# Start-up fill issued by two engines, maxima by pairs in the lone batches, and feed-forward chunks two places later, in an attention plus feed-forward kernel

## What is computed

```python
Q, K, V = (proj(W) for W in (Wq, Wk, Wv))      # 16 heads of 16, T = 512
att = einsum('bhqd,bhkd->bhqk', Q, K) * 0.25 + b
att = softmax(att * m + (1 - m) * -1e30)
y = einsum('bhqk,bhkd->bhqd', att, V)          # back to [8, 256, 512]
gate, up = y @ Wg.T, y @ Wu.T                  # Wg, Wu [4096, 512], Wd [512, 4096]
out = x + (gelu_tanh(gate) * up) @ Wd.T        # packed 4-bit codes times block scales
```

## Time and profile before

| what | us |
|---|---|
| median of 3 runs (1523.91 to 1530.12) | 1525.85 |
| the profiled execution | 1526.61 |
| its span, first to last instruction | 1524.8 |
| first scores of batch 0 | 62.3 |
| first gate matmul of chunk 0 | 221.8 |
| PE busy over the span | 1421.5 (93%) |
| mean granted TensorE clock, share of full | 0.966 |

### The profile page before, as it was taken

How to read it: one execution, slowest core, us unless ns; L and a number is a source line. 1 busy time by engine, 2 the same in 40 slices (tenths; PEclk the granted TensorE clock), 3 DMA queues, 4 the chain that set the end, 5 groups by cost and what they waited for, 6 DMA issues and landing times.

```text
span 1524.8 us, 18901 instructions
## 1 busy us (share of the span) xinstructions
PE 1421.5 (93%) x7376; PEld 555.1 (36%) x7376; DVE 698.3 (46%) x934; ACT 752.1 (49%) x855; POOL 309.6 (20%) x242
## 2 busy tenths in 40 slices
PE   3688779999999998999999998999999999999998
PEld 1122223333333333333433333333333334444443
DVE  5667668777778753433344333433343111111111
ACT  2255558666667663555665554556655631111110
POOL 3002024433444421111211111111111111111110
PEclk7589989999999999999999999999999999999999
DMA  5130324443354332432243320432222223233220
GB/s 182 51 87 15 101 78 163 154 131 122 108 183 157 133 125 65 143 99 84 84 128 106 101 84 20 155 119 83 84 84 83 84 83 138 83 126 123 83 84 28
DMA packets 51129, 157.91 MB, mean 104 GB/s; under 512 B 7632, under 2 KB 21072, under 8 KB 50912
## 3 DMA queue, kind: packets, MB, share of 16 engines
q1 hardware_dynamic: 48192, 153.80, 29.5%
q10 hardware_dynamic: 2848, 2.90, 0.6%
HBM read 118.64 MB, written 37.77 MB: 103 GB/s over the span
## 4 chain that ended last, share of the span: by engine, by line
PE 81%; DMA 4%; DVE 3%; ACT 3%; issue 3%; POOL 2%; SPq 2%; ACTq 1%; POOLq 0%; DVEq 0%
PE psum L896 14%; PE psum L897 13%; PE psum L898 13%; PE psum L944 8%; PE psum L945 7%; PE psum L946 7%; PE psum L866 7%; PE psum L852 4%; PE psum L836 4%; PE psum L812 2%; DMA wide<-seed_rows 2%; POOL dq_w L400 1%; DVE w_ring L414 1%; PE psum L822 1%; ACTq L393 1%
## 5 line engine op out<-in xcount | busy, mean ns | idle before, releaser
L633 ACT ACTIVATE big<-psum 128x1024 f32<-128x1024 f32 x256 | 260.1, 1024 | 328.4 <-PE psum L852 321.4
L896 PE MATMUL psum<-y_hi,w_ring 128*128 128x512 f16 x1024 | 390.5, 381 | 16.5 <-POOL y_lo L515 15.8
L898 PE MATMUL psum<-y_hi,w_ring 128*128 128x512 f16 x1024 | 389.6, 380 | 0.0
L897 PE MATMUL psum<-y_lo,w_ring 128*128 128x512 f16 x1024 | 389.4, 380 | 0.0
L700 DVE TENSOR_REDUCE maxima<-psum 128x2 f32<-128x1024 f32 x179 | 219.2, 1225 | 253.6 <-PE psum L836 253.3
L527 POOL TENSOR_TENSOR in_lo<-inter,in_hi 128x512 f16<-128x512 f32 x128 | 150.4, 1175 | 811.1 <-ACT in_hi L615 810.5
L748 DVE SCALAR_TENSOR_TENSOR inter<-psum,gelu 128x512 f32<-128x512 f32 x128 | 88.2, 689 | 315.4 <-PE psum L898 301.4
L944 PE MATMUL psum<-w_ring,in_hi 128*128 128x512 f16 x512 | 195.5, 382 | 7.7 <-ACT gelu L608 4.3
L945 PE MATMUL psum<-w_ring,in_hi 128*128 128x512 f16 x512 | 194.8, 380 | 0.0
L946 PE MATMUL psum<-w_ring,in_lo 128*128 128x512 f16 x512 | 194.6, 380 | 0.0
L896 PEld LDWEIGHTS psum<-y_hi,w_ring 128*128 128x128 f16 x1024 | 100.1, 98 | 202.6 <-issue 82.7
(11 more groups left out here) (69 smaller groups left out, 987.3 us busy)
## 6 DMA issues: line engine op xcount, KB each, us to landing
w_ring<-w_parts SPq DMA_DIRECT2D x96, 768.0 KB, 7.2
w_parts<-w_ring SPq DMA_DIRECT2D x32, 768.0 KB, 3.3
dq_scales<-scales SPq DMA_DIRECT2D x32, 384.0 KB
wide<-qk_parts SPq DMA_DIRECT2D x64, 128.0 KB
qk_parts<-wide SPq DMA_DIRECT2D x60, 128.0 KB
dq_packed<-packed SPq DMA_DIRECT2D x32, 192.0 KB
small<-x SPq DMA_DIRECT2D x8, 512.0 KB, 6.6
wide<-qk_parts SPq DMA_DIRECT2D x64, 64.0 KB
```

The lines of the kernel that those rows point to most:

```text
L633: nc.scalar.activation(p_exp[:, k, :, i], p_score[:, bank:bank + 2, :], ACT.Exp, scale=SCORE_SCALE).then_inc(exp_done, 1)
L896: nc.tensor.matmul(dst, w[:, 0, k % 2, cols], hi, start=(k == 0), stop=False)
L897: nc.tensor.matmul(dst, w[:, 0, k % 2, cols], lo, start=False, stop=False)
L898: return nc.tensor.matmul(dst, w[:, 1, k % 2, cols], hi, start=False, stop=(k == TT - 1))
```

## The change

1. **Start.** The loads of feed-forward units 0 and 1 go behind the first `move_max`; the 1792 KB mask load and its reduction go, in their place 8 values (`any_b`) go to DRAM and back to all partitions. ACT makes one tiny copy early. K's store of unit 0 goes to ACT; the first fill no longer waits for V and `x_lo`, and its ten DMAs are issued half by SP and half by ACT, after ACT's three weight splits. Fill of unit 1 comes right behind, once the first has landed (before: step `F1`). `weight_f`, `weight_hi`, `weight_lo` and `decode` of unit 0 leave the start and go into batch 0.
2. **Lone batches.** `PLAN` gets the order of `SHARED_PLAN` without places; maxima by pairs in the same two banks (4 and 5), scores stay in four. `F0` goes from the third quad to the second, `G1` from the fourth to the third. Batch 1 now decodes units 1 and 2, batch 0 unit 0.
3. **Chunks.** Each chunk starts behind the second `|` after that `YN`; two places are added at the end.
4. **End.** The last group's down products run unit by unit (i outside, r inside), and down waits for each unit's `in_lo` by itself.

```diff
         PLAN = (
-            "F1 A2 m A3 m AO m S00 S01 V1a m m S10 V1b V1h m S11 m Y S20 MT MH XH YN m m ML S21 MV A0 m m A1 m "
-            "S30 m S31 m Q0a m Q0b m Q0h Q0l",
...
-            "S00 m S01 d2 m A2 m m V0b S10 V0h m m A3 m AO S11 m MT m S20 m Y YN MH m ML U G1 S21 MV m S30 A0 m S31 m "
-            "A1 m wh m wl",
+            "S00 m m A2 V1a S01 m m A3 V1b V1h AO S10 m m XH S11 m m d10 MT Y MH ML YN d11 S20 m m A0 Q0a MV d12 S21 m m "
+            "Q0b Q0h h1 S30 m m A1 Q0l K0a S31 m m K0b K0h K0l l1",
+            "X F0 S00 m m A2 Q1a S01 m m A3 Q1b Q1h AO S10 m m Q1l S11 m m MT Y MH ML YN S20 m m A0 MV K1a S21 m m "
+            "K1b K1h S30 m m A1 K1l S31 m m",
+            "G1 S00 m m A2 d00 d20 S01 m m A3 AO S10 m m d01 d21 S11 m m MT Y MH ML YN d02 d22 S20 m m A0 MV L2 S21 m m V0a "
+            "S30 m m h0 h2 A1 V0b V0h S31 m m l0 l2",
+            "S00 m m A2 S01 m m A3 AO S10 m m S11 m m MT Y MH ML YN S20 m m A0 MV L3 S21 m m S30 m m A1 S31 m m",
         )
...
-            for step in "| A2 | A3 | AO | | Y | YN".split():
+            for step in "| A2 | A3 | AO | | Y | YN | |".split():
...
-                for r in range(4):
-                    for i in range(GROUP):
+                for i in range(GROUP):
+                    for r in range(4):
                         yield STEPS, "D", (STEPS // GROUP - 1, r, i)
...
-            ready = [n + 1 for n, (b, g, step, _) in enumerate(steps) if step == "YN" and g == 0 and b >= 2 and b % 2 == 0]
+            ready = []
+            for n, (b, g, step, _) in enumerate(steps):
+                if step == "YN" and g == 0 and b >= SOLO and b % 2 == 0:
+                    places = [m for m in range(n, len(steps)) if steps[m][2] == "|"]
+                    ready.append(places[1] + 1)
...
-            load_unit(sp, 0)
-            load_unit(sp, 1)
+            sp.wait_ge(dve_own, 2)
+            sp.dma_start(any_dram, any_b).then_inc(any_out, 16)
             sp.wait_ge(setup, 4)
             sp.wait_ge(fixed, 2)
             sp.dma_start(seed_dram, seed).then_inc(seed_out, 16)
             store_qk(sp, 0, 0, 0)
-            store_qk(sp, 0, 0, 1)
+            sp.wait_ge(seed_out, 16)
+            sp.wait_ge(qk_out[0], 64)
+            fill_half(sp, 0, 0, 0, 0)
+            store_qk(sp, 0, 1, 0)
+            store_qk(sp, 0, 1, 1)
+            sp.wait_ge(stack_in[0], 16 * STACK_DMAS)
+            fill_stack(sp, 0, 0, 1, False)
             sp.wait_ge(x_lo_s, 1)
             sp.wait_ge(v_proj, 1)
             load_x(sp, 1)
-            sp.wait_ge(seed_out, 16)
-            fill_stack(sp, 0, 0, 0, False)
+            sp.wait_ge(any_out, 16)
+            sp.dma_start(any_key[:, :], any_dram.rearrange("b o -> (b o)").partition_broadcast(P)).then_inc(any_in, 16)
             move_max(sp, 0, 0, 0)
+            load_unit(sp, 0)
+            load_unit(sp, 1)
...
             act.wait_ge(any_set, 1)
-            for u in range(2):
-                for side in range(2):
-                    qk_part(0, side, u, True, psum[:, 2 * u + side, :])
+            for side in range(2):
+                qk_part(0, side, 0, True, psum[:, side, :])
+            store_qk(act, 0, 0, 1)
+            for side in range(2):
+                qk_part(0, side, 1, True, psum[:, 2 + side, :])
+            for i in range(3):
+                act.wait_ge(proj_in[i], 16)
+                nc.scalar.activation(w_parts[i][0], w_proj[i], ACT.Copy, scale=W_SCALE).then_inc(wp_hi_s, 1)
+            act.wait_ge(seed_out, 16)
+            act.wait_ge(qk_out[0], 64)
+            fill_half(act, 0, 0, 0, 1)
...
             def down(j, r, i):
                 u = GROUP * j + i
+                if r == 0:
+                    pe.wait_ge(in_lo_s, u + 1)
                 if i == 0:
-                    if r == 0:
-                        pe.wait_ge(in_lo_s, GROUP * j + GROUP)
```

More of the change, by code:

```diff
@@ L133, in up_bank, with score_bank @@
             return psum[:, 1 if u > LAST_CHUNK and u % 2 else 3, :]
+        def score_bank(b, i):
+            return 2 * i if b < SOLO else 0
         def out_bank(j, r):
@@ L147, in build @@
         dve_own = sem("dve_own")
+        act_own = sem("act_own")
+        warm_in = sem("warm_in")
         any_set = sem("any_set")
@@ L240, in plan @@
                     continue
-                if step == "F1" and not first:
+                if step[0] in "dhl" and (step[1] == "0") != first:
+                    continue
+                if step == "L2" and not first or step == "L3" and first:
                     continue
@@ L540, in _ @@
                     x_low(b + 1)
-                elif step == "d2" and b < SOLO:
-                    weight_f(pool, b + 1)
+                elif step in ("d02", "d12", "d22") and b < SOLO:
+                    weight_f(pool, int(step[1]))
         @block.scalar
@@ L591, in _ @@
             x_high(0)
-            for i in range(3):
-                act.wait_ge(proj_in[i], 16)
-                nc.scalar.activation(w_parts[i][0], w_proj[i], ACT.Copy, scale=W_SCALE).then_inc(wp_hi_s, 1)
-            store_qk(act, 0, 1, 0)
-            store_qk(act, 0, 1, 1)
-            weight_hi(act, 0)
             max_part(0, 0, True)
@@ L621, in _ @@
                         inter_high(u - 1)
-                    elif step == "G1" and SOLO < u + AHEAD_UNITS - 1 < UNITS:
+                    elif step == "G1" and AHEAD_UNITS <= u + AHEAD_UNITS - 1 < UNITS:
                         weight_hi(act, u + AHEAD_UNITS - 1)
@@ L649, in _ @@
                     x_high(b + 1)
-                elif step == "wh" and b < SOLO:
-                    weight_hi(act, b + 1)
+                elif step in ("h0", "h1", "h2") and b < SOLO:
+                    weight_hi(act, int(step[1]))
         @block.vector
         def _(dve):
+            nc.vector.memset(act_warm[:, :], 0.0).then_inc(warm_in, 1)
             for e in range(2):
@@ L765, in _ @@
                         decode(dve, n, int(step[1]))
-                    elif step == "G3" and SOLO < n - 1 < UNITS:
+                    elif step == "G3" and AHEAD_UNITS <= n - 1 < UNITS:
                         weight_lo(dve, n - 1)
@@ L786, in _ @@
                 elif step[0] == "d" and b < SOLO:
-                    decode(dve, b + 1, int(step[1]))
-                elif step == "wl" and b < SOLO:
-                    weight_lo(dve, b + 1)
+                    decode(dve, int(step[1]), int(step[2]))
+                elif step in ("l0", "l1", "l2") and b < SOLO:
+                    weight_lo(dve, int(step[1]))
         @block.tensor
@@ L847, in scores @@
                     pe.wait_ge(max_in, 16 * MAX_DMAS * (4 * b + g) + 16 * MAX_DMAS)
+                if (b, g, k, i) == (0, 0, 0, 1):
+                    pe.wait_ge(qk_lo, 4)
                 wait_from(pe, exp_done, n - 1 if b < SOLO else n)
-                bank = 2 * i if b < SOLO else 0
                 for e in range(2):
                     rows, s = slice(HALF * e, HALF * e + STACK_ROWS), 2 * g + i
-                    last = nc.tensor.matmul(p_score[:, bank + e, :], k_stack[rows, side, s, k * P:(k + 1) * P],
+                    last = nc.tensor.matmul(psum[:, score_bank(b, i) + e, :], k_stack[rows, side, s, k * P:(k + 1) * P],
                                             q_stack[rows, side, s, :], start=True, stop=True)
```

102 lines of the change are left out of this document (43 added, 59 removed), and 4 rows, old and new, of the table PLAN.

## The result

The changed kernel takes 1530.86 us (median, 1528.01 to 1535.98) where the kernel before, run beside it, takes 1526.22: ratio 1.0032, 95% interval 1.0021 to 1.0042. The forecast was 1496. It is slightly slower, not 2% faster. Its profiled execution has a span of 1530.9 us, the one of before 1524.8, so 6.1 us have to be found.

What follows compares the result with a forecast made beforehand. PE was taken as the bound from 221.8 us, with only its waits to save. Gains of 7.2 + 3.1 - 0.6 + 14.4 + 1.7 + 4.3 = 30.1 gave 1496 us against the median, range 1489 to 1504.

Steps and rivals of the forecast that it cites:

- The step that failed: Shared stretch from 221.8 us: PE is the bound and only its waits can be saved; inside chunk 0 no loss was forecast.
- Lone batches: Batches 0 and 1 were to take 69.5 and 71.5 us against 72.55 and 70.94: gain 3.1 and -0.6.
- Rival A: Lone batches: the pair's round trip leaves PE waiting in every step and brings half clock, slower; chance 0.03 in full.
- Rival B: Lone batches: clock swings in a third of the stage or DVE's extras cost double, batches of 77, 1510 us; chance 0.16.
- Rival C: First fill limited by the issuer, so 2.4 us sooner, and lone batches of 66.5: 1486 us; chance 0.13.
- rival D: Chunk starts don't fill and the `y_lo` wait only moves, so 12 us come back: 1508 us; chance 0.05.
- First gate: Start of chunk 0: a score step, one pair and A0 go into the 4.75 us wait, gain 1.7.
- Start: Up to the second transpose of maxima: earlier first fill, then costlier pairs, second transpose at 65.6 not 72.80, gain 7.2.
- the second issuer: First fill issued by two engines: saves at most 2.4 us of issue time, and nothing was taken for it.
- Chunk starts: Chunks 1 to 3: the wait for `y_lo` is filled by feed-forward steps of the chunk before, gain 14.4.
- End: Last group's down products: PE no longer waits 2.72 us for `in_lo` nor restarts at half clock, gain 4.3.
- PE's waits in the shared stretch: Sign of a wrong prediction: these waits growing beyond the 4 us in 320 of before.

Runs made afterwards that it cites:

- e1: Changed kernel with part 3 undone, every chunk starting right behind YN again: 1520.03 us, ratio 0.9961 to the kernel before.
- e3: Kernel before with part 3 alone, chunks starting two places later: 1536.53 us, ratio 1.0068 to the kernel before.
- e5: Changed kernel with chunk 0 starting right behind YN and keeping its old step counts, chunks 1 to 3 still later: 1509.24 us, ratio 0.9896.
- e12: Changed kernel with lone pairs in four banks, chunks three places later, unit 1 decoded in batch 0's last quad: 1484.22 us, ratio 0.9722.
- e7: Changed kernel with maxima one tile at a time in the start and lone batches: 1516.23 us, ratio 0.9928 to the kernel before.
- e9: Changed kernel with lone maxima by pairs in turn in four banks, scores in two: 1513.53 us, ratio 0.9923 to the kernel before.
- e8: Changed kernel with both halves of the first fill issued by SP alone: 1532.44 us (one run).
- e4: Changed kernel with POOL splitting y at step S21, not YN, in quads from batch 2 on that start no chunk: 1524.95 us, ratio 0.9995.

## Why the prediction was wrong, step by step

In the spans the forecast was 30.1 us less and the measurement is 6.1 more, 36.2 apart: 21.7 and 1.7 in and ahead of chunk 0, 8.7 in the lone batches, 3.1 inside chunks 1 and 2, 2.0 at the chunk starts, less the start, better by 0.9, and the end, by 0.1.

1. **The step that failed.** It is the sentence "Nothing in the change removes a feed-forward matmul, so there only its waits can be saved". It says what can be gained and was used as if it said what can be lost. Part 3 moves 368 steps of chunk 0 by six against the attention's steps, and with them the order on DVE, POOL and ACT. I priced the two places at the ends of chunks and left the inside of chunk 0 unpriced, no bound either. The earlier trace rows lie in chunk 1 or later, where PE is the bound; chunk 0 still decodes weights and is another stage, with PE idle 14.3 us in 308. e1, e3 and e5 show that part 3's new order in chunk 0 is the cause.
2. **Lone batches, mis-sized.** Forecast 69.5 and 71.5, measured 71.4 and 78.35. For batch 0 the miss is within the spread of executions (68.9 to 71.8), for batch 1 it is not (74.4 to 78.4). The round trip was seen and its price of 2.0 in the start was right (2.03), but "DVE's other work fits into the 0.57 that each round trip leaves it idle" was not. With one pair in flight, what DVE does between two reductions can stop PE: from 64 to 220 us PE waits for maxima 27.0 us. It shows most in the quad with unit 1's decode, 23.4 us long (136.06 to 159.49), where a quarter of the forecast's 71.5 is 18. That quad is no shorter with single tiles (23.8), 1.6 shorter with pairs in four banks (21.8) and 19.3 with four banks and the decode moved away (e12), so DVE's work there, and not the round trip alone, was priced too low. The 14.6 and 17.3 us that e7 and e9 take off are not the size of this miss either, since 7.7 and 11.5 of them come in the start, which was forecast right with the pairs as they are. A small slip goes the same way: 9 steps of 2.3 and 23 of 1.8 are 62.1, not 61.5.
3. **Rival A** (half clock throughout) did not come: 0.88 and 0.83 in the two batches, 0.66 in the last quad alone. **Rival B** was the nearest for this part, with batches of 77 against a mean of 74.9. The means of 0.88 and 0.83 lie between the 0.50 of the first quad's maxima and the 1.00 of a quad of batch 0, but so do the 0.86 and 0.90 of the kernel before (its batches 0 and 1), and e9, with a second buffer, has 0.85 in batch 0. No run here shows that the pairs in two banks brought the lower clock. **Rival C** fell with e8, **rival D** with the `y_lo` row.
4. **First gate.** 1.7 was forecast and at the marker nothing came: from the second transpose of batch 2 to the first gate it takes 219.88 - 214.41 = 5.47, before 221.76 - 216.29 = 5.47, since the gate comes when POOL's `y_lo` does. PE's wait went from 4.75 to 1.12, with other work in it. That work is not lost: when unit 0's marker comes, the changed kernel has done a score, a pair and a product with V more (226.49 to 228.03, 1.5 us) and a piece of a projection. The gain then stands in a later row of the table.
5. **Start** right: first tile 31.19 (forecast 32.6), transposes 47.50 and 64.68 (48.9 and 65.6), pair 2.03 (2.0), gain 8.1 (7.2). Nothing for the second issuer was right as well.
6. **Chunk starts** nearly right: 12.4 for 14.4. As the work moved at the first gate comes back in here, it is fairer to take the two terms together, 12.4 for 16.1.
7. **End** right, 4.4 for 4.3. The last stretch, changed kernel:

```profile
1525.65 2.63 DVE L768 SCALAR_TENSOR_TENSOR acc<-psum,acc 128x512 f32<-128x512 f32 x4 [7.67 <-PE psum L955]
```

The four adds come together, as forecast.

The prediction named what would make it wrong: PE's waits in the shared stretch growing beyond those of the earlier trace rows. Taken by its rows the test misses the loss, since from 860 to 1180 us the changed kernel's PE is busy 318.69 of 320 us, more than the 315.85 of before; it had to be read for chunk 0, and no rival had that stage. A rival "the moved steps meet others" could have been made from the trace of before: steps of a place, places of a quad and the order on DVE around `y_f` all stand there.

## What to carry to other kernels

Where one in-order schedule is laid over another at a fixed rate, work out the period of both: if they are locked, a shift by a few steps changes every meeting in the stage and is an edit of its own, to be priced there and not only at the ends. Try the neighbouring shifts, since here two places cost 22 us inside chunk 0 and three places 2. Merge small instructions on the consumer's side only if the producer keeps a second buffer: over the start and two batches, pairs in two banks were 15 to 17 us slower than singles in two or pairs in four. And take the profile of one execution for what it is: the same steps of the two lone batches took 143.3 us in one and 149.7 in another.

## What was new about the hardware

- **POOL and DVE hold each other up.** POOL's `y_hi` (0.39 us alone) and `y_lo` (0.67) last 1.05 and 2.06 when DVE's OR or low part runs, each of which reads two tensors in SBUF. The rows at 350 us fit a plain block: `w_ring` ends at 351.18 + 1.95 = 353.13, and `y_lo`, begun at 351.60, ends at 353.66, 0.53 later; the OR ends at 351.26 and `y_hi` at 351.51, 0.25 later. Both are 0.14 less than the instruction lasts alone. It goes the other way too: the decode's first shift takes 1.23 instead of 0.35 beside POOL's `in_lo` (347.40 to 348.56). That shift has one input, where the OR and the low part have two. That the one instruction waits for the end of the other is the author's estimate from these times; no run shows what it waits for. e4 puts a price on most of it: 5.9 us for six quads.
- **Five DMAs from each of two engines land when ten from one do**: the first tile starts at 31.19 and 31.07, although the last issue was some 2 us later in the second (at 24.21 in e8, by 22.3 in the changed kernel).
